# Cross-attention maxima from the keys' high halves, two products at a time in the array's two 64-row halves, with the score operands laid out anew

## The reference

```python
qh = (q @ Wq).reshape(B, N, NUM_HEADS, HEAD_DIM).transpose(0, 2, 1, 3)
kh = (kv @ Wk).reshape(B, M, NUM_HEADS, HEAD_DIM).transpose(0, 2, 1, 3)
vh = (kv @ Wv).reshape(B, M, NUM_HEADS, HEAD_DIM).transpose(0, 2, 1, 3)
scores = jnp.einsum('bhnd,bhmd->bhnm', qh, kh) * scale
attn = jax.nn.softmax(scores, axis=-1)
out = jnp.einsum('bhnm,bhmd->bhnd', attn, vh)
out = out.transpose(0, 2, 1, 3).reshape(B, N, INNER)
return out @ Wo + bo
```

## Time and profile before

| | before |
|---|---|
| runs | 4041.73, 4039.97, 4037.01 us, median 4039.97 |
| profiled execution, span | 4037.7 us |
| TensorE, matmuls busy | 3793.1 us, 94% |
| VectorE busy | 3135.7 us, 78% |
| ScalarE busy | 2674.0 us, 66% |
| GpSimd busy | 2544.9 us, 63% |
| mean granted TensorE clock | 0.954 of 2.4 GHz |

### The profile page before, as it was taken

The page is one execution under the profiler, slowest core; times in us unless marked ns, Lnnn a source line. Parts: engine busy times, 40 slices in busy tenths (PEclk is TensorE's granted clock), DMA queues, the critical chain, the costliest instruction groups (busy, mean ns, idle before and its releaser), DMA issues.

```text
span 4037.7 us, 110587 instructions
## 1 busy us (share of the span) xinstructions
PE 3793.1 (94%) x43467; PEld 2886.6 (71%) x43467; DVE 3135.7 (78%) x6499; ACT 2674.0 (66%) x5365; POOL 2544.9 (63%) x2457
## 2 busy tenths in 40 slices
PE   6999999989969999999799999996997899999987
PEld 4777777766637777777577777775765677777765
DVE  6999999858978888888577888886654788888864
ACT  4888887756637777777467777773442577777752
POOL 4888888759856776767456676675001476676761
PEclk8999999979989999999699999998998899999988
DMA  4333333125432222121112212110000212122100
GB/s 129 104 110 112 110 108 107 41 92 158 143 100 61 57 60 61 54 61 49 28 54 62 59 54 64 57 54 21 3 1 18 64 54 64 57 59 61 55 22 15
DMA packets 157328, 266.80 MB, mean 66 GB/s; under 512 B 26632, under 2 KB 97432, under 8 KB 155432
## 3 DMA queue, kind: packets, MB, share of 16 engines
q1 hardware_dynamic: 156360, 259.67, 22.5%
q10 hardware_dynamic: 448, 0.06, 0.0%
HBM read 165.10 MB, written 50.26 MB: 53 GB/s over the span
## 4 chain that ended last, share of the span: by engine, by line
PE 87%; DVE 6%; POOL 2%; ACT 2%; DMA 1%; issue 1%; SPq 1%; POOLq 0%; DVEq 0%; ACTq 0%
PE ps L186 83%; PE ps L659 1%; DVE xn L166 1%; POOL wst L539 1%; PE ps L242 1%; PE ps L255 1%; PE ps L1638 1%; DVE wst L817 1%; DVE wst L772 0%; PE ps L1160 0%; DVE st L151 0%; DMA big<-big 0%; DVE relu L769 0%; DMA ynN<-cx 0%; ACT wb L324 0%
## 5 line engine op out<-in xcount | busy, mean ns | idle before, releaser
L539 POOL TENSOR_TENSOR wst<-wst 125x384 bf16<-125x384 f32 (+1 forms) x1536 | 1432.0, 932 | 843.4 <-ACT wst L745 783.1
L745 ACT ACTIVATE wst<-ps 125x448 f32<-125x448 f32 x3072 | 1518.5, 553 | 569.3 <-PE ps L186 554.8
L186 PE MATMUL ps<-big,cx 128*125 128x448 bf16 (+1 forms) x6144 | 1428.8, 354 | 0.8 <-DMA big<-topT 0.8
L186 PEld LDWEIGHTS ps<-cx,wst 125*128 125x128 bf16 x23040 | 1113.5, 98 | 307.5 <-POOL wst L539 15.2
L817 DVE TENSOR_TENSOR wst<-wst 125x512 bf16<-125x512 f32 (+1 forms) x1536 | 1269.4, 827 | 56.8 <-ACT wst L745 56.5
L186 PE MATMUL ps<-cx,wst 125*128 125x65 bf16 (+2 forms) x23040 | 1202.4, 204 | 12.1 <-POOL wst L539 11.6
L186 PEld LDWEIGHTS ps<-big,cx 128*125 128x125 bf16 (+1 forms) x6144 | 835.1, 137 | 284.2 <-issue 1.8
L186 PE MATMUL ps<-cx,big 128*128 128x500 bf16 (+1 forms) x2688 | 709.4, 317 | 10.2 <-DVE big L1743 2.6
L772 DVE TENSOR_REDUCE wst<-ps 128x1 f32<-128x500 f32 x896 | 603.9, 674 | 136.6 <-PE ps L186 123.9
L769 DVE CUSTOM_DVE_ANT_0 wst<-ps,wst 128x500 bf16<-128x500 f32 x448 | 302.6, 676 | 207.2 <-PE ps L186 150.8
L769 DVE CUSTOM_DVE_ANT_0 relu<-ps,relu 128x500 bf16<-128x500 f32 x448 | 301.8, 674 | 147.8 <-PE ps L186 84.1
(11 more groups left out here) (250 smaller groups left out, 4260.2 us busy)
## 6 DMA issues: line engine op xcount, KB each, us to landing
big<-big SPq DMA_DIRECT2D x768, 56.0 KB, 2.7
cx<-ctxT SPq DMA_DIRECT2D x96, 375.0 KB, 3.5
cx<-ctxN SPq DMA_DIRECT2D x64, 377.9 KB
cx<-in_ctxN SPq DMA_DIRECT2D x64, 375.0 KB
cx<-ctxT SPq DMA_DIRECT2D x96, 187.5 KB, 3.8
ctxN<-cx SPq DMA_DIRECT2D x32, 377.9 KB
ynN<-cx SPq DMA_DIRECT2D x32, 377.9 KB
cx<-ynN SPq DMA_DIRECT2D x32, 377.9 KB
```

Source lines behind the costliest of these rows:

```text
L186: return t.matmul(o, l, r, start=start, stop=stop, skip_group_check=True)
L539: g.tensor_tensor(pl[r][0:KP, at:], pf[r][0:KP, at:], pf[r][0:KP, at:].bitcast(BF16)[:, 1::2], ALU.subtract).then_inc(s["plp"], 1)
L745: e.activation(pf[T % 3][0:KP, cols], bank(2 + n2 % 3, 448)[0:KP], ACT.Exp, scale=scale).then_inc(s["ev"], 1)
```

## The change

A product for a maximum now contracts 64 rows: high keys with high queries, without the low keys. `cs` holds the keys' high halves in both row halves, and `diff` with it. Most products come in pairs, one on array rows 0 to 63 and one on rows 64 to 127, in two banks. The program marks these instructions as 64-row tiles of the array, at row positions 0 and 64. `PLAN` has nine pairs and three single products for each sequence; a single one (`r3`, `s6`, `r6`) contracts 128 rows as before. A group stands at one place of the step, before the scores. It takes both of the banks 0 and 1, and waits until both products of the group before have been read (for the first sequence of an attention, the group two before).

The score operands are laid out so that the four score matmuls contract 128 rows each: `Q1` has queries' high halves over low halves, `Q2` has the shift in row 0, zeros and the high halves in rows 64 to 127; `chx` has ones in row 0, zeros, and the low keys in rows 64 to 127. POOL writes the zeros. Keys are loaded in two transfers of 64 rows in place of one of 128. A pair `r1`,`r2` or `r4`,`r5` is reduced by one DVE instruction in place of two. Query positions, score tiles, value products and everything outside the cross-attentions stay.

```diff
-        PLAN = (("d0", "s0"), ("r0", "d1"), ("s1", "d2"), ("r1", ""), ("s2", "r2"), ("d3", "s3"),
-                ("r3", "d4"), ("s4", "d5"), ("r4", "s5"), ("r5", "d6"), ("s6", ""), ("r6", ""))
+        PLAN = (("d0", "r0"), ("d1", "s0"), ("r1", "r2"), ("d2", "s1"), ("d3", "s2"), ("r3",),
+                ("d4", "s3"), ("d5", "s4"), ("r4", "r5"), ("d6", "s5"), ("s6",), ("r6",))
+        TILES = (slice(0, 64), slice(64, 128))
...
-            for r in (0, 64):
-                y.dma_start(Qh[r:r + 64, o, 0:HQ // 2], qch[u][0:64]).then_inc(s[f"qd_{u}"], 16)
+            for of, rows in ((Q1, TILES[0]), (Q2, TILES[1])):
+                y.dma_start(of[rows, o, 0:HQ // 2], qch[u][0:64]).then_inc(s[f"qd_{u}"], 16)
...
+        def wait_max_banks(w, kb, k, n):
+            of = n - 1 if k else n - 2
+            w.wait_ge(s["half"], NJ * kb + through(of, "d") if of >= 0 else NJ * kb)
+            w.wait_ge(s["red"], maxima(kb, of) if of >= 0 else 2 * NJ * kb)
...
-                    y.dma_start(cs[i], srcT[k]).then_inc(s[f"lT_{i}"], 16)
+                    for rows in TILES:
+                        y.dma_start(cs[i][rows, :], srcT[k][0:64]).then_inc(s[f"lT_{i}"], 16)
...
+            g.memset(big[0:64, 7168:7168 + QB * HQ // 2], 0.0).then_inc(s["zo"], 1)
...
-                mm(t, bank(max_bank(b0 + k, k, item), 500), Qh[:, k % QB, 128 * j:128 * j + 128],
-                   diff[:, :] if kind == "d" else cs[k % 3][:, 500 * c:500 * c + 500], True, True).then_inc(s["mxm"], 1)
+                wait_max_banks(w, b0 + k, k, n)
+                for u, item in enumerate(items):
+                    c, j = PARTS[item[0]], int(item[1])
+                    rows = TILES[u] if len(items) == 2 else slice(0, 128)
+                    r = mm(t, bank(max_bank(k, n, u), 500), (Q1, Q2)[u][rows, k % QB, 128 * j:128 * j + 128],
+                           diff[rows, :] if c == 0 else cs[k % 3][rows, 500 * c:500 * c + 500], True, True)
+                r.then_inc(s["mxm"], len(items))
...
-                        mm(t, o, cs[k % 3][:, keys], Qh[:, k % QB, cols], True, False)
+                        mm(t, o, cs[k % 3][:, keys], Q1[:, k % QB, cols], True, False)
                         wait_shift(w, ci, k)
-                        wait_spread_low(w, ci, k)
-                        mm(t, o, chx[k % 2][:, keys], Ql[0:65, k % QB, cols], False, True).then_inc(s["sc"], 1)
+                        mm(t, o, chx[k % 2][:, keys], Q2[:, k % QB, cols], False, True).then_inc(s["sc"], 1)
...
+                if len(items) == 2 and items[0][0] == "r":
+                    j, at = int(items[0][1]), 512 * max_bank(k, n, 0)
+                    of = ps[:, at:at + 1024].rearrange("p (u n) -> p u n", u=2)[:, :, 0:500]
+                    v.tensor_reduce(to[:, j:j + 2, 1], of, AX.X, ALU.max).then_inc(s["red"], 2)
+                    return
```

More of the change, by code:

```diff
@@ L356, in turns, with through, group_of, maxima @@
             k, n = divmod(T + 17, KT)
-            return [(k, PLAN[n])] if 0 <= k < B else []
-        PLAN = (("d0", "s0"), ("r0", "d1"), ("s1", "d2"), ("r1", ""), ("s2", "r2"), ("d3", "s3"),
-                ("r3", "d4"), ("s4", "d5"), ("r4", "s5"), ("r5", "d6"), ("s6", ""), ("r6", ""))
-        ORDER = tuple(i for two in PLAN for i in two if i)
+            return [(k, n)] if 0 <= k < B else []
+        PLAN = (("d0", "r0"), ("d1", "s0"), ("r1", "r2"), ("d2", "s1"), ("d3", "s2"), ("r3",),
+                ("d4", "s3"), ("d5", "s4"), ("r4", "r5"), ("d6", "s5"), ("s6",), ("r6",))
+        ORDER = tuple(i for group in PLAN for i in group)
         PARTS = {"d": 0, "s": 1, "r": 2}
-        def before(item, kinds):
-            return sum(i[0] in kinds for i in ORDER[:ORDER.index(item)])
-        def halves(kb, item):
[L368 to L378, removed]
+        TILES = (slice(0, 64), slice(64, 128))
+        def through(n, kinds):
+            return sum(i[0] in kinds for group in PLAN[:n + 1] for i in group)
+        def group_of(item):
+            return next(n for n in range(KT) if item in PLAN[n])
+        def halves(kb, item):
+            return NJ * kb + int(item[1])
+        def maxima(kb, n):
+            return 2 * NJ * kb + through(n, "sr")
+        def products(kb, n):
+            return len(ORDER) * kb + through(n, "dsr")
+        def max_bank(k, n, u):
+            return u if k else 2 * (n % 2) + u
         def place(h):
@@ L606, in pe_cross @@
                     n2 += 1
-                for k, items in turns(T):
-                    if items[0]:
-                        product(k, items[0])
+                for k, n in turns(T):
+                    products_of(k, n)
                 if 0 <= T < NT:
@@ L685, in high, with relu @@
                 e.activation(qch[k % 2], bank(7, 448), ACT.Copy).then_inc(s["pa"], 1)
[L687 to L693 removed]
+            def relu(k, n):
+                kb, item = b0 + k, PLAN[n][0]
+                w.wait_ge(s["mxm"], products(kb, n))
+                h, j = halves(kb, item), int(item[1])
+                if h >= 2:
+                    w.wait_ge(s["red"], maxima(kb, group_of(f"s{j - 2}")) if j >= 2 else maxima(kb - 1, group_of(f"s{j + NJ - 2}")))
+                e.activation(relus[h % 2], bank(max_bank(k, n, 0), 500), ACT.Relu).then_inc(s["half"], 1)
             high(0)
@@ L735, in act_cross @@
                                  ACT.Copy).then_inc(s["oc"], 1)
-                for k, items in turns(T):
-                    if items[0][0:1] == "d":
-                        relu(k, items[0])
+                for k, n in turns(T):
+                    if PLAN[n][0][0] == "d":
+                        relu(k, n)
                 if 0 <= T < NT:
@@ L746, in act_cross @@
                         n2 += 1
-                for k, items in turns(T):
-                    if items[1][0:1] == "d":
-                        relu(k, items[1])
         NEXT_NORM = (1, 3, 5, 11)
```

98 lines of the change are left out of this document (39 added, 59 removed).

## The result

| | before | after |
|---|---|---|
| runs | 4037.01 to 4041.73 us, median 4040.72 of 4 | 4083.52 to 4089.79 us, median 4085.93 of 4 |
| profiled execution, span | 4037.7 us | 4081.7 us |
| mean granted TensorE clock | 0.954 | 0.949 |

The changed kernel is slower: the ratio is 1.0116, with a 95% interval of 1.0101 to 1.0130. That is 45 us, where +69 was predicted.

The account below looks back on a forecast made before the run. PE was taken to bound the kernel. Pairs +56, waits +10, query transfers +4 and saved reductions -1 gave +69 us on a span of 4037.7, or 4107; with the median 2.3 higher, 4109 us, range 4030 to 4240.

Parts of the forecast that it names:

- the likeliest case: Whole kernel slower, as the terms sum: 4109 us, own range 4070 to 4200; chance 0.63.
- What bounds the kernel: PE streams columns all the time in the attentions; its gains or losses are the kernel's while DVE's 8% slack lasts.
- What a pair saves: On PE, two products of 0.212 us stream as one: 0.212 less for each of 1096 pairs.
- the halves don't work at once: In a pair, the second product streams behind the first: 0.25 us more a pair, kernel 4325; chance 0.07.
- What a pair adds: On PE, tiling changes and second load make a pair 0.475 us against 0.424: +56 us, bounds +39 to +146.
- faster: Tiling changes on PE are cheaper in bf16 than in the rows read; about 3820 if both are free; chance 0.13.
- My other value there: If one of a pair's two tiling changes on PE is free, -101 + 13 gives 3950 us.
- The scores: "so nothing": Score matmuls on 128 rows in place of 65 keep their 0.19 us each, so no change.
- The new waits: Groups wait for both earlier products' readers, tightest at groups 8 to 11 in attention 0: +10 us, between 0 and 60.
- the readers set the pace: PE waits for both banks at each sequence, DVE lacking its 0.2 us: 4161, up to 4220; chance 0.10.
- Small things: At attention starts, query low halves' transfers +4 us, fewer reductions -1; key transfers and 128-row scores nothing.
- The signs: PE timeline: pair starts within 0.1 us, load at pair's end less 0.07, L716 about 23.4, full clock, DVE idle grows.

Follow-up runs that it names:

- the lone 64-row products: Kernel before with three of a sequence's 21 products (r1, s6, r6) on 64 rows, without a pair: 4130.88 us, ratio 1.0220.
- full-row run: Changed kernel with every product on all 128 rows, so no 64-row tiles; order, groups, waits, layouts and transfers kept: 4092.23 us, ratio 1.0128.

## Why the prediction was right, and where it was off

The direction and the likeliest case were right: two changes of tiling cost more than the halves save. By its own steps:

*What bounds the kernel*: right. PE is busy in 649 of 650 us after, 650 before. Four edits to its stream (both products on one half, the pair twice, the lone 64-row products, the 128-row scores) moved the time by their count times their size. It holds only while the readers keep up: with full rows, waits took back the 41 us that PE's stream gained, and with the groups behind the scores they took back what the exposed loads had left of the gain.

*What a pair saves*, 0.212: right, shown by the two products on one half (+0.216 each) and by the second pair (+0.211). The rival that the halves don't work at once falls.

*What a pair adds*: mechanism right, size 15 us too large. Entering was worked out at 0.317 and measured at 0.314, leaving at 0.334 and 0.333. The second load was put at 0.015 and is 0.003, and the ordinary score to be subtracted is 0.189, not 0.191. So the pair is 0.461 and not 0.475, and the term +41 and not +56 us. The rule of the Trainium skill (TensorEngine Tiling (Array Packing), Key Properties), that a change of tiling mode drains the engine, holds by the trace: 0.33 against 0.19 at each leaving, the next load at the pair's end each time. The other rule of the Trainium skill that I weighed (TensorE: Matmul & The Clock Gate, Measured speedup vs the span model), about 4 ns for a further tile, agrees for the tile itself, with 3 ns here; taken as the whole cost, as in the rival "faster", it was 266 us off, since it counts no change of mode. My other value there, 3950 with one change free, holds for leaving alone; with entering alone free the same sum gives 3994.

*The scores: "so nothing"*. This is the step that failed. Rows of 128 and 65 in turn cost 2.3 ns for each score matmul. The two decimals of the earlier trace rows can't show that, and I had put it down to the 3 ns that every matmul takes. It is -14 us, shown by itself in the kernel before (-13).

*The new waits*, +10: right in size, 8 to 10 us by the trace of the changed kernel, but not a small matter. Without the pairs the same order waits for 54 us. The place was half right. In the changed kernel the products wait in attention 0, once in two sequences, at `s6` (group 10, inside the groups 8 to 11 that I worked out) and as often at `d2` (group 3, behind a double reduction), 1.7 and 1.2 us in 28 sequences. In the other attentions a value matmul comes 0.11 late once in two sequences, and the rest is in each attention's first sequences. Without the pairs it is the group behind each double reduction, in all attentions, where I had seen no issue. The rival that the readers set the pace didn't come true, but the full-row run says that with a faster PE it would have, and the rival "faster" left that out.

*Small things*: +3 expected and +4 measured, from the distances of L717 across the attentions' starts.

*The signs*: the products of a pair start 3 ns apart, the next load starts at the pair's end less 0.07, and the clock stays full, as said. L716's distance is 23.19 and not 23.4, and from the last value matmul's start to the first score's it is 0.44 and not 0.48. One sign was wrong: DVE's idle time grew in attention 0 alone. In attention 1 DVE is busy for 535 us of 650 where it was for 528.

The sum is 41 - 14 + 10 + 4 = 41, against 44 in the span; the 3 that are left I can't place.

The forecast was 24 us too high, and two errors that point the same way make that up: 15 us too much for the pairs, and the scores' 14 us left out. The waits' 10 us were a guess between 0 and 60, and that they came out right is luck: I had not seen that this order waits for 54 us as soon as the pairs' slower step is gone. Why a change of row count costs 2.3 ns is open too; only that it does is shown.

## What to carry to other kernels

Work in 64-row tiles pays only when it stands together: here a change in and out costs 0.25 us (0.105 + 0.144), a pair gains 0.21, and two pairs in one visit would gain 0.42. That is PE's time alone: no run had two pairs of different products in one visit, which would need four banks and readers that keep up. Before trading PE time, take the PE work away by itself and look at what waits then: an order that looks free beside a slower stream may cost as much as the stream saves. And give the neighbours in a long stream of matmuls the same number of rows, with zeros where need be: that was the only kind of edit here that gained, 7 to 14 us of 4040.

## What the runs showed of the hardware that was not expected

- A score matmul whose neighbour has another number of rows (65 or 96 beside 128) takes 191.5 ns from end to end, with equal rows (128 and 128, or 96 and 96) 189.1 to 189.3. At four in each of 1536 steps that is 14 us of 4040.
- Two 64-row weight loads on the two halves start together (both at 1288.56 in the changed kernel), and the second product ends 3 ns behind the first.
- A weight load of 125 columns takes 137 ns against 97 for 128. A score matmul with such a load ends 216 ns behind a 65-column matmul, and 189 behind a 448- or 500-column one.
- The load engine's idle time at a change of tiling is listed as a wait for whichever semaphore came last (201 us for ACT in the page of the changed kernel), though nothing waited for ACT.
